# Loading every fourth group of the first edge layer during the node stage before it

## What is computed

```python
h = relu(layernorm(x))
Wh = h @ W + b
# layer 0: edges (row = src, col = dst)
sim = cosine(Wh[row], Wh[col])
base = edge_weight * softplus(...) * (row != col)
x = x + scale * (c0 * segment_sum(base * relu(sim) * Wh[col], row)
                 - c1 * segment_sum(base * relu(-sim) * Wh[col], row) + c2 * Wh)
# layer 1
h = relu(layernorm(x))
msgs = mlp(concat(h[dst], h[src]))
agg = segment_sum(msgs, dst)
x = x + mlp(concat(h, agg))
```

## Time and profile before

| | us |
|---|---|
| median of 3 runs (lowest, highest) | 2410.95 (2409.88, 2411.21) |
| profiled execution: its own time | 2418.68 |
| its span, first to last instruction | 2416.6 |
| POOL busy | 1695.9 (70%) |
| PE busy | 1562.8 (65%) |
| DVE busy | 1553.3 (64%) |
| ACT busy | 864.0 (36%) |

### The profile page before, as it was taken

How to read it: one execution, slowest core, us unless ns; L and a number is a source line. 1 busy time by engine, 2 the same in 40 slices (tenths; PEclk the granted TensorE clock), 3 DMA queues, 4 the chain that set the end, 5 groups by cost and what they waited for, 6 DMA issues and landing times. The chain is left out here.

```text
span 2416.6 us, 57279 instructions
## 1 busy us (share of the span) xinstructions
PE 1562.8 (65%) x16004; PEld 1340.6 (55%) x16004; DVE 1553.3 (64%) x5636; ACT 864.0 (36%) x3093; POOL 1695.9 (70%) x1413
## 2 busy tenths in 40 slices
PE   4886755455555555555555550005999999997998
PEld 2555645455554545545455550004999999994554
DVE  5995655555555454554545552794999999995554
ACT  3773322222222222222222221462333333334665
POOL 2775888888888888888888886746777777761322
PEclk9996555555555555555555555556999999999999
DMA  3775544444444444444444432565555454534664
GB/s 100 251 247 172 114 82 80 77 83 75 84 79 78 84 74 85 80 77 83 75 86 73 84 47 18 170 221 146 128 124 126 124 126 124 126 81 119 188 188 145
DMA packets 342563, 273.11 MB, mean 113 GB/s; under 512 B 144834, under 2 KB 273514, under 8 KB 342484
## 3 DMA queue, kind: packets, MB, share of 16 engines
q1 hardware_dynamic: 259028, 233.22, 33.2%
q0 software_dynamic: 81536, 38.61, 15.0%
q10 hardware_dynamic: 1920, 0.37, 0.1%
HBM read 206.69 MB, written 65.34 MB: 113 GB/s over the span
## 5 line engine op out<-in xcount | busy, mean ns | idle before, releaser
L1117 POOL DMA_INDIRECT x<-e_sums,e_to x392 | 623.4, 1590 | 126.4 <-issue 118.6
L1352 PE MATMUL bank<-e_parts,e_same 128*128 128x64 bf16 x2940 | 172.8, 240 | 586.7 <-DVE e_parts L1211 586.7
L1304 PE MATMUL bank<-e_window,e_onehot 128*128 128x64 f32 x2352 | 525.0, 422 | 16.8 <-DMA e_window<-wh 16.8
L1304 PEld LDWEIGHTS bank<-e_window,e_onehot 128*128 128x128 f32 x2352 | 511.7, 332 | 16.9 <-DVE e_onehot L1143 16.9
L1102 POOL DMA_INDIRECT e_ends<-wh,e_ids x392 | 425.2, 1085 | 132.8 <-issue 102.1
L1352 PEld LDWEIGHTS bank<-e_parts,e_same 128*128 128x128 bf16 x2940 | 159.4, 129 | 602.8 <-issue 602.8
L829 POOL DMA_INDIRECT e_near_source<-h,e_near_ids x392 | 394.8, 1007 | 129.8 <-issue 117.4
L1250 ACT ACTIVATE e_sq<-e_ends 128x64 f32<-128x64 f32 x784 | 188.6, 241 | 686.0 <-DMA e_ends<-wh,e_ids 685.9
L1175 DVE SCALAR_TENSOR_TENSOR e_prod<-e_ends 128x64 f32<-128x64 f32 x392 | 65.7, 223 | 370.8 <-DMA e_ends<-wh,e_ids 370.8
L939 PE MATMUL bank<-e_near_to_edge,e_near_window 128*64 128x128 f32 x2352 | 153.4, 281 | 171.2 <-DMA e_near_window<-h 171.2
L939 PEld LDWEIGHTS bank<-e_near_to_edge,e_near_window 128*64 128x64 f32 x2352 | 130.0, 139 | 177.6 <-DVE e_near_to_edge L850 171.6
(11 more groups left out here) (150 smaller groups left out, 2860.9 us busy)
## 6 DMA issues: line engine op xcount, KB each, us to landing
e_window<-wh SPq DMA_DIRECT2D x392, 96.0 KB
e_near_window<-h SPq DMA_DIRECT2D x392, 96.0 KB
e_owners<-ends SPq DMA_DIRECT2D x98, 256.0 KB, 2.9
n_x<-x SPq DMA_DIRECT2D x98, 256.0 KB, 3.0
n_x<-in_x_dram SPq DMA_DIRECT2D x49, 256.0 KB, 2.8
wh<-n_wh SPq DMA_DIRECT2D x49, 256.0 KB, 2.0
x<-n_x SPq DMA_DIRECT2D x49, 256.0 KB, 2.3
e_rel<-rel SPq DMA_DIRECT2D x98, 128.0 KB, 3.2
```

Source lines behind the costliest of these rows:

```text
L1117: pool.indirect_dma_start(out=added_tab, out_offset=bass.IndirectOffsetOnAxis(ap=t.to[s][:, j:j + 1], axis=0), in_=t.sums[s][:, j, :], in_ ...
L1304: last = nc.tensor.matmul(bank[s % 2][:, j * D:(j + 1) * D], onehot, window, start=w == 0, stop=w == WK - 1)
L1352: last = nc.tensor.matmul(bank[6 + s % 2][:, i * D:(i + 1) * D], t.same[s][:, same_block(j, i), :], t.parts[s][:, part, j, :], start=j == ...
```

## The change

A group whose number is 3 modulo 4 (slot AHEAD = 3) among the first 96 groups is loaded ahead: 24 groups (AHEADS), 96 tiles. During node_phase0 POOL issues their indirect DMAs on the raw input x into a tile `ahead` of 24 KB per partition: 6 at the stage's start and then 8 for every 5 blocks (`gather_ahead`). Two such groups make a block of 128x512, and the 12 (EXTRA) blocks so made are numbered 49 to 60. They pass through the same norm, transpose and product, but ACT writes the product back to `ahead`, and nothing of them is added or stored. In the edge layer ACT copies the rows of such a group from `ahead` to t.ends (in `found`), a semaphore `copied` stands for the gathered one, and POOL's gathers of the other three groups are spread over the four steps of a round, 3 a step.

To make room on POOL in node_phase0, `begin_x1` and ACT's n_part are gone: DVE makes x1 in one instruction from n_wh, the coefficient and x (`add_x`), and h is split as it already is in node_phase1, the first 5 of 8 rows on DVE (`dve_h_of`) and the last 3 on ACT (`act_h`, 3 instructions of 64 columns). POOL's program in this stage is written out instead of looped.

The diff, cut to its core:

```diff
+AHEAD = ESLOTS - 1
+AHEADS = GROUPS // ESLOTS
+EXTRA = AHEADS * G // R
...
+            extra_in=[ctx.enter_context(nc.semaphore(f"n0_extra_in{i}")) for i in range(EXTRA)],
...
-        node_phase0(nc, c, tabs, x)
-        first, second = c["sems"], Semaphores(nc)
-        c["sems"] = second
-        edge_phase(nc, c, tabs, layer=0, done=first)
+        with ExitStack() as early:
+            c["ahead"] = early.enter_context(nc.sbuf_tensor("ahead", [P, AHEADS, G, D], FP32))
+            node_phase0(nc, c, tabs, x)
+            first, second = c["sems"], Semaphores(nc)
+            c["sems"] = second
+            edge_phase(nc, c, tabs, layer=0, done=first)
...
-def rounds_of_blocks(eng, parts, slots=0, blocks=0):
+def rounds_of_blocks(eng, parts, slots=0, blocks=0, full=0):
...
-    full = blocks // slots
+    full = full or blocks // slots
...
+def extra(s, k):
+
+    return isinstance(k, int) and k * SLOTS + s >= BLOCKS
+
+
+def extra_rows(c, s, k):
+
+    i = k * SLOTS + s - BLOCKS
+    return c["ahead"][:, 2 * i:2 * i + 2].rearrange("p g j d -> p (g j d)")
...
+    def source(self, s, k):
+        return rows(extra_rows(self.c, s, k) if extra(s, k) else self.x[s][:])
+
     def dve_total(self, dve, s, k):
-        dve.wait_ge(self.x_in[s], 16 * (k + 1))
-        self.nc.vector.tensor_reduce(self.total[s][:], rows(self.x[s][:]), AX.X,
+        if extra(s, k):
+            dve.wait_ge(self.extra_in[k * SLOTS + s - BLOCKS], 16 * R)
+        else:
+            dve.wait_ge(self.x_in[s], 16 * (k + 1))
+        self.nc.vector.tensor_reduce(self.total[s][:], self.source(s, k), AX.X,
...
+            if self.h_act_ready:
+                pool.wait_ge(self.h_act_ready, count(s, k, SLOTS))
+        self.nc.gpsimd.tensor_tensor(rows(self.xc[s][:]), self.source(s, k), by_row(self.mean[s][:]),
                                      ALU.subtract).then_inc(self.xc_ready, 1)
...
-                ln.dve_h(dve, s, k)
-
-            rounds_of_blocks(dve, [(-2, squares), (0, mean), (-2, normed)])
+                ln.dve_h_of(dve, s, k, SPLIT)
+
+            def add_x(s, k):
+                if extra(s, k):
+                    return
+                dve.wait_ge(wh_ready, count(s, k))
+                if began(k):
+                    dve.wait_ge(stored[s], 32 * k)
+                nc.vector.scalar_tensor_tensor(x1[s][:], wh[s][:], c["mix"][:, 2:3], ln.x[s][:], ALU.mult,
+                                               ALU.add).then_inc(x1_ready, 1)
+
+            rounds_of_blocks(dve, [(-2, squares), (0, mean), (-6, add_x), (-2, normed)], SLOTS, BLOCKS + EXTRA, ROUNDS)
 
         @block.gpsimd
         def _(pool):
-            def begin_x1(s, k):
-                pool.wait_ge(wh_ready, count(s, k))
-                pool.wait_ge(x1_part, count(s, k))
-                if began(k):
-                    pool.wait_ge(stored[s], 32 * k)
-                nc.gpsimd.tensor_tensor(x1[s][:], part[s][:], ln.x[s][:], ALU.add).then_inc(x1_ready, 1)
-
-            rounds_of_blocks(pool, [(-1, lambda s, k: ln.pool_centre(pool, s, k)), (-6, begin_x1)])
+            rows_ahead = [(i, r) for i in range(EXTRA) for r in range(R)]
+
+            def gather_ahead(start, end):
+                for i, r in rows_ahead[start:end]:
+                    g, j = 2 * i + r // G, r % G
+                    pool.indirect_dma_start(
+                        out=c["ahead"][:, g, j, :], out_offset=None, in_=x,
+                        in_offset=bass.IndirectOffsetOnAxis(ap=c["edge_i"][:, 0, ESLOTS * g + AHEAD, j:j + 1], axis=0),
+                    ).then_inc(ln.extra_in[i], 16)
+
+            gather_ahead(0, 6)
+            for n in range(BLOCKS + EXTRA):
+                ln.pool_centre(pool, n % SLOTS, n // SLOTS)
+                gather_ahead(6 + 8 * n // 5, 6 + 8 * (n + 1) // 5)
...
             def copy_wh(s, k):
                 act.wait_ge(wh_done, count(s, k))
+                if extra(s, k):
+                    nc.scalar.copy(extra_rows(c, s, k), wh_bank[s % 2][:]).then_inc(wh_ready, 1)
+                    return
                 if began(k):
                     act.wait_ge(stored[s], 32 * k)
                 nc.scalar.copy(wh[s][:], wh_bank[s % 2][:]).then_inc(wh_ready, 1)
+
+            def normed(s, k):
                 if began(k):
-                    act.wait_ge(x1_ready, count(s, k, SLOTS))
-                nc.scalar.activation(part[s][:], wh_bank[s % 2][:], ACT.Copy, scale=c["mix"][:, 2:3]).then_inc(x1_part, 1)
+                    act.wait_ge(turned, count(s, k, SLOTS))
+                ln.act_h(act, s, k, range(SPLIT, R))
 
             rounds_of_blocks(act, [(-3, copy_hT), (-2, lambda s, k: ln.act_std(act, s, k)),
-                                   (-1, lambda s, k: ln.act_square(act, s, k)), (-5, copy_wh)])
+                                   (-1, lambda s, k: ln.act_square(act, s, k)), (-5, copy_wh), (-2, normed)],
+                             SLOTS, BLOCKS + EXTRA, ROUNDS)
...
+                pe.wait_ge(ln.h_act_ready, count(s, k))
...
-                    pe.wait_ge(x1_part, count(s, k, 2))
...
-            rounds_of_blocks(pe, [(-3, turn), (-4, multiply)])
+            rounds_of_blocks(pe, [(-3, turn), (-4, multiply)], SLOTS, BLOCKS + EXTRA, ROUNDS)
...
+    def is_ahead(self, s, near):
+
+        return near and self.layer == 0 and s == AHEAD
+
     def all_gathered(self, eng, s, k, near):
 
+        if self.is_ahead(s, near):
+            eng.wait_ge(self.copied, k + 1)
+            return
         eng.wait_ge(self.gathered[s], 16 * G * (1 if near else 2) * (k + 1))
...
+    def gather_rows(s, k, j):
+        if j == 0:
+            pool.wait_ge(t.ids_ready, count(s, k, 0, ESLOTS))
+            if has(s, k, ESLOTS, ESLOTS):
+                pool.wait_ge(t.ends_used, count(s, k, ESLOTS, ESLOTS))
+            pool.sem_inc(t.waited, 1)
+        for end, at in ((0, t.src_at), (1, t.dst_at))[:1 if near else 2]:
+            pool.indirect_dma_start(
+                out=t.ends[s][:, j, at, :], out_offset=None, in_=gathered_tab,
+                in_offset=bass.IndirectOffsetOnAxis(ap=t.ids[s][:, end, j:j + 1], axis=0),
+            ).then_inc(t.gathered[s], 16)
+
     def gather(s, k):
-        pool.wait_ge(t.ids_ready, count(s, k, 0, ESLOTS))
-        if has(s, k, ESLOTS, ESLOTS):
-            pool.wait_ge(t.ends_used, count(s, k, ESLOTS, ESLOTS))
-        pool.sem_inc(t.waited, 1)
-        for j in range(G):
-            for end, at in ((0, t.src_at), (1, t.dst_at))[:1 if near else 2]:
-                pool.indirect_dma_start(
-                    out=t.ends[s][:, j, at, :], out_offset=None, in_=gathered_tab,
-                    in_offset=bass.IndirectOffsetOnAxis(ap=t.ids[s][:, end, j:j + 1], axis=0),
-                ).then_inc(t.gathered[s], 16)
+        if layer == 0 and near:
+            last = isinstance(k, int) and k * ESLOTS + s == GROUPS - 1
+            share = AHEAD * G // ESLOTS
+            for n in range(share * s, G * (s + 1) if last else share * (s + 1)):
+                gather_rows(n // G, k, n % G)
+        else:
+            for j in range(G):
+                gather_rows(s, k, j)
...
     def found(s, k):
-        act.wait_ge(t.found, count(s, k, 0, ESLOTS))
         if has(s, k, ESLOTS, ESLOTS):
             act.wait_ge(t.ends_used, count(s, k, ESLOTS, ESLOTS))
+        if t.is_ahead(s, near):
+            nc.scalar.copy(t.ends[s][:, :, t.src_at, :],
+                           c["ahead"][:, bass.ds(k, 1), :, :].rearrange("p g j d -> p (g j) d")).then_inc(t.copied, 1)
+        act.wait_ge(t.found, count(s, k, 0, ESLOTS))
         nc.scalar.copy(t.ends[s][:, :, t.dst_at, :],
```

More of the change, by code:

```diff
@@ L427, in rounds_of_blocks @@
         steps(k)
-    for k in range(full, full + first + 1):
+    for k in range(full, blocks // slots + first + 1):
         steps(k)
@@ L469, in __init__ @@
     def __init__(self, nc, c, slots, h):
-        self.nc, self.c, self.h = nc, c, h
+        self.nc, self.c, self.h, self.h_act_ready = nc, c, h, None
         self.x, self.xc, self.sq = (slots.bufs(n, [P, R * D]) for n in ("x", "xc", "sq"))
```

16 lines of the change are left out of this document (9 added, 7 removed).

## The result

Median 2358.78 us of four runs (2341.68, 2354.18, 2363.38, 2369.23), beside 2411.08 for the kernel before on the same chip (four runs, 2409.88 to 2413.36): ratio 0.9761, 95% interval 0.9733 to 0.979. The change saves 52 us where 81 were forecast; 2358.78 lies in the range, 29 us above the number. The profiled execution is the fastest, 2341.68 us, 77.0 less than the profiled execution before, which itself lies 7.6 above its median. The four runs spread over 28 us, those of before over 3.5, and TensorE's mean granted clock was 0.708 in the fastest and 0.694 to 0.696 in the others.

The account below looks back on a forecast made before the run. POOL's instruction stream was taken to bound the edge layer, DVE lengthened by POOL the node stage. -130 + 49 = -81 us gives 2338 against the profiled 2418.68, or 2330 for the median; range 2306 to 2372.

Parts of the forecast that it names:

- Edge layer, -130 forecast: First edge layer: 92 gathers leaving POOL save 1.39 us each, plus 2.7 us at the start, 130 us in all.
- The cover of three gathers: Edge layer: three gathers, 4.2 us, between two runs of scatters still cover the scatters' landing, for which POOL waited 2.50 us.
- Rival 2: Edge layer: three gathers no longer cover landings or ACT's order, a quarter of the saving lost, 2362 us; chance 0.09.
- Node stage, +49 forecast: node_phase0: +2 at the start, +13 for 40 blocks, +39 for 12 extra blocks, -5.5 at the end.
- The forecast for one block, 3.5 us: node_phase0: a later block takes 3.5 us instead of 3.17, between 3.28 and 3.95, as DVE and POOL hold each other.
- My lower bound, ACT's loop of 3.28: node_phase0: ACT's last piece of h, the transposes and ACT's idle time before n_hT keep a block at least 3.28 us.
- rival 1: Node stage: gathers get dearer, 1.63 us plus 0.30 each, making POOL the bound, 35 us more, 2365; chance 0.12.
- rival 4: Node stage: each gather of x waits for the one ahead to land, 141 us more, 2471, slower; chance 0.06.
- Taken strictly: Node stage: the DVE and GpSimd port lock excludes whole instructions, so a block takes about 3.6 us, 2334 in all.
- rival 3: Node stage: TensorE loses its higher clock, a block takes 4.86 us, 73 us more, 2403; chance 0.05.
- the baseline: Whole kernel: the median of three runs, 2410.95, lies 7.7 us below the profiled execution, so the forecast was lowered to 2330.

Follow-up runs that it names:

- e4_unspread: The changed kernel with the edge layer's remaining gathers not spread: four in each of three steps, none in the fourth; 2801.8 us, ratio 0.995.
- e2_filled: The changed kernel plus one unread matmul of 256 columns per node-stage block from the ninth on; 2747.66 us, ratio 0.9774.
- e6_filled: The changed kernel plus one unread matmul of 256 columns per node-stage block, on the third chip; 2339.9 us, ratio 0.9669.
- e3_room_only: The changed kernel with only the room made on POOL: nothing loaded ahead, no extra blocks, edge layer as before; 2837.73 us, ratio 1.0083.
- e11_plain: e6_filled with the 96 gathers of x replaced by 12 plain loads of other rows, so results differ from the reference; 2336.12 us, ratio 0.9676.
- e9_act_first: The kernel with the unread matmul, with ACT's copy of n_wh put ahead of its copy of n_hT; 2341.37 us, ratio 0.9695.
- e7_order: e6_filled with DVE's squares' sum put between mean and add_x, and one more row of 64 on DVE; 2355.13 us, ratio 0.9728.
- e5_again: The changed kernel unedited, on the third chip; 2349.8 us, ratio 0.9713.
- e1_again: The changed kernel unedited, on another chip where the kernel before takes 2824.31 us; 2765.91 us, ratio 0.9785.
- run 17: Not a run's label: the words say that the lower clock cost 17 us in the longest run of e1_again, 2786.24 us.
- e8_room_filled: e3_room_only plus the unread matmul per node-stage block; 2424.26 us, ratio 1.0026.
- e10_apart: e9_act_first with DVE also reordered, two sums beside POOL's subtraction, and the unread matmul cut to 128 columns; 2337.12 us, ratio 0.9686.

## Why the prediction was right and where it was wrong

**Edge layer, -130 forecast, -126 measured.** The gathers gave more and the scatters took some back. Of the gathers' group 113.9 us of busy time and 28.9 of idle time (without e_ids) went: 142.8 / 96 = 1.49 us each, where 1.39 had been taken. The scatters lengthened from 1.590 to 1.621 us in the mean, 12 us over 392, and wait 7.7 us more; waits for e_ids behind the first gather are 3 us shorter. At the start 1.8 us were saved where 2.7 had been taken, since the first scatter now waits for e_to. The cover of three gathers held: the scatters' waits for landed ones are 7.6 us in all, which is the last three groups, where no gathers are left. e4_unspread shows what hangs on it: POOL waits 63 us for landings when one step in four is bare. Rival 2 did not come.

**Node stage, +49 forecast, +50.9 in the profiled execution.** Its terms: the first subtraction 2.8 us later (forecast 2), the ninth to the 49th 141.3 us instead of 126.9, +14.4 (13), twelve extra blocks 39.6 (39), the end 16.6 instead of 20.4, -3.7 (-5.5), and -2.2 from the first to the ninth, which I had left as it was. The forecast for one block, 3.5 us, is right with the clock held: 3.48 in e2_filled, 3.47 in e6_filled (subtractions 19 to 49). It consists of 3.36 for the room made (e3_room_only, e11_plain) and 0.11 for gathers. My lower bound, ACT's loop of 3.28, was no bound of this kernel (e9_act_first); that the extra blocks, 3.30, agree with it is chance: the first six, which still run beside add_x, take 3.5, the last six 3.1. A gather of x takes 1.00 us, and 1.21 with the idle time before it (the 21.6 us ahead of the first left out), not 1.39, and rival 1 is out. POOL was not held up by landings either: gathers of x follow each other after 0.30 us, and rival 4 is out.

**The lock.** add_x and n_h hold the subtraction and are held by it, as the earlier trace rows showed for n_h alone. The Trainium skill ("SBUF — State Buffer", section "SBUF: two separate sides") says that either excludes the other for its whole length, and this trace agrees: n_h of 320 columns ends 0.35 us after the subtraction, add_x of 512 in e7_order 0.55 us after, 0.14 and 0.20 less than each takes alone. Taken strictly it gave 3.6 us a block; measured are 3.48.

**The step that failed is rival 3.** I gave TensorE's lower clock 0.05 and priced it as all or nothing, 4.86 us for each of 52 blocks and 2403 in all, arguing from one row of before, 57% busy at 0.83, that 78% was "well above". Measured is something in between: the clock falls for some 3 to 38 us at a time, one to several times a run. In the profiled run it cost about 2 us (3.53 instead of 3.48 a block), in e5_again some 7 (3.65), in e1_again's longest run 17 (3.92). Nor was the busy share the thing to argue from. In the changed kernel the clock fell after stretches with PE busy 84 to 85%, but from 106 to 246 us of the trace above it held at 79 to 85%; filled, it fell after 94% in e8_room_filled and after 99% in e10_apart. The filling held it from 36 to 256 us in e2_filled, e6_filled and e11_plain, not in e7_order, e8_room_filled, e9_act_first and e10_apart. What makes it fall stays open.

**The 29 us between the number and the median.** Some 12 of them lie between the forecast and the fastest run: 4 are the terms above, and 7.7 are the baseline, for I took the changed kernel's profiled execution to lie as far above its median as that of before did, and it is the fastest of its four. The other 17 lie between the fastest run and the median, and the three longer runs have no trace. Their mean clocks and spans come to 60 to 80 us more at 1.2 GHz than in the fastest; at the 15 us that 51 more such us cost in e1_again, an estimate, that is 19 to 24 us, where they are 12, 22 and 28 longer. So the clock, which I had left at nothing, is probably most of those 17, but where in the program it fell in them isn't shown. The filling agrees: with it the same change is worth 78.6 us on the third chip (e6_filled) where 81 were forecast, and 68.7 without, and the spread of 18 us is 4. It does not prove that all of this is the node stage: of the 10.9 us between those two traces 3.2 lie there, and the edge layer, 1169.6 to 1178.0 in traces of the same program for it, varies by 8 us of itself.

## What to carry to other kernels

Work taken out of a stage's bound engine is worth what its own timeline says, and it pays to ask what the removed instructions covered: here spreading the rest over the gap was two fifths of the stage's gain. When an edit thins out PE in a stage where it runs at its higher clock, price the clock as stretches, not as all or nothing, and try a cheap matmul that nobody reads; then look at the clock in the trace, since the matmul held it in three of seven traces here. Before moving a held instruction, look at who will be held in its place, and at the loads that wait for it.
